# A two-layer graph network on one core: GpSimd gathers rows for phase two in the pause between the phases, from a list split by how early a row is ready

## The reference

```python
# layer 0: attention over the edges that enter a node
hi = x[src] @ w1;  hj = x[tgt] @ w2
logits = (leaky_relu(hi + hj, 0.3) * a).reshape(-1, 8, 16).sum(-1)
attn = softmax of logits over the edges with one tgt        # segment max, exp, segment sum
x = layernorm(x + segment_sum(hi * attn, tgt))
# layer 1: a message for every edge
ef = (relu(edge_attr @ We1 + be1) @ We2 + be2) * sigmoid(edge_weight * Wt + bt)
msg = relu(concat(x[src], ef) @ Wn1 + bn1) @ Wn2 + bn2
x = layernorm(x + (segment_sum(msg, dst) + x))
```

## Time and profile before

| | us |
|---|---|
| median of 3 runs | 2163.57 (2163.52, 2163.57, 2169.5) |
| the profiled execution | 2166.06 |
| its span in the trace | 2164.1 |
| GpSimd busy | 1585.8 (73%), 1679 instructions |
| TensorE matmul busy | 1630.1 (75%) |
| VectorE busy | 1312.3 (61%) |
| ScalarE busy | 645.3 (30%) |

### The profile page before, as it was taken

How to read it: one execution, slowest core, us unless ns; L and a number is a source line. 1 busy time by engine, 2 the same in 40 slices (tenths; PEclk the granted TensorE clock), 3 DMA queues, 4 the chain that set the end, 5 groups by cost and what they waited for, 6 DMA issues and landing times.

```text
span 2164.1 us, 39852 instructions
## 1 busy us (share of the span) xinstructions
PE 1630.1 (75%) x10499; PEld 1256.3 (58%) x10500; DVE 1312.3 (61%) x3313; ACT 645.3 (30%) x1376; POOL 1585.8 (73%) x1679
## 2 busy tenths in 40 slices
PE   5766766766676766766678778888888888888886
PEld 5554544545454554544556566666666666666665
DVE  5766667666776676767643355555555555555554
ACT  5211111111111111111133444344444344444442
POOL 6777777777777777777547777777777777777775
PEclk8999989899999899999989988988988988888897
DMA  8633333333333333333354344444444444444441
GB/s 261 150 86 86 84 96 91 95 86 96 97 86 96 88 93 92 94 94 89 88 165 140 126 127 143 129 138 132 128 144 128 130 142 128 142 130 141 129 130 45
DMA packets 145935, 252.48 MB, mean 117 GB/s; under 512 B 34549, under 2 KB 80874, under 8 KB 145882
## 3 DMA queue, kind: packets, MB, share of 16 engines
q1 hardware_dynamic: 92122, 142.56, 20.3%
q0 software_dynamic: 53184, 109.03, 19.4%
q10 hardware_dynamic: 576, 0.25, 0.1%
HBM read 233.91 MB, written 13.02 MB: 114 GB/s over the span
## 4 chain that ended last, share of the span: by engine, by line
POOL 59%; issue 23%; DVE 6%; PE 6%; DMA 3%; DVEq 1%; POOLq 1%; ACT 1%; SPq 0%; ACTq 0%
POOL T L712 33%; POOL G L680 26%; DMA G<-hi_rows,idx 2%; PE ps L1789 1%; PE ps L1812 1%; PE ps L1784 1%; DMA T<-y_rows,idx 1%; DVE msg L1285 1%; PE ps L1742 1%; DMA accF<-in_x_turned 1%; DVE oh L1338 0%; ACT V L848 0%; DVE V L1257 0%; DVEq L1262 0%; DVE G L1600 0%
## 5 line engine op out<-in xcount | busy, mean ns | idle before, releaser
L712 POOL DMA_INDIRECT T<-y_rows,idx x831 | 787.7, 948 | 295.4 <-issue 292.1
L680 POOL DMA_INDIRECT G<-hi_rows,idx x819 | 781.7, 954 | 261.1 <-issue 245.5
L1784 PE MATMUL ps<-ident,G 128*128 128x128 f32 x828 | 143.1, 299 | 287.0 <-DMA G<-hi_rows,idx 182.2
L2014 PE MATMUL ps<-wA,G 128*128 128x128 f32 x1664 | 266.1, 310 | 97.6 <-DVE T L1556 97.3
L949 ACT ACTIVATE G<-G 128x512 f32<-128x512 f32 x208 | 131.1, 630 | 595.7 <-DVE G L1600 594.2
L2014 PEld LDWEIGHTS ps<-wA,G 128*128 128x128 f32 x1664 | 232.3, 216 | 103.3 <-DVE G L1604 103.2
L848 ACT ACTIVATE V<-ps 128x512 f32<-128x512 f32 x207 | 123.7, 597 | 561.5 <-PE ps L1789 553.1
L1784 PEld LDWEIGHTS ps<-ident,G 128*128 128x128 f32 x828 | 94.9, 150 | 337.1 <-issue 298.1
L1596 DVE TENSOR_TENSOR G<-iotaF,R 128x256 f32<-128x256 f32 x208 | 88.6, 426 | 296.8 <-DMA T<-y_rows,idx 292.7
L1812 PE MATMUL ps<-msg,oh 128*128 128x137 f32 x1608 | 264.8, 313 | 0.3 <-issue 0.3
L1257 DVE TENSOR_TENSOR V<-ps,V 128x512 f32<-128x512 f32 x207 | 142.0, 686 | 201.6 <-ACT V L848 199.6
(11 more groups left out here) (201 smaller groups left out, 1701.5 us busy)
## 6 DMA issues: line engine op xcount, KB each, us to landing
T<-in_edge_weight_padded SPq DMA_DIRECT2D x104, 512.0 KB
T<-in_edge_attr_turned SPq DMA_DIRECT2D x104, 256.0 KB
Dbc<-block_destinations SPq DMA_DIRECT2D x69, 384.0 KB, 3.8
T<-y_rows,idx POOLq DMA_INDIRECT x831, 2.5
G<-hi_rows,idx POOLq DMA_INDIRECT x819
link<-scan_destinations SPq DMA_DIRECT2D x280, 16.1 KB
accF<-in_x_turned SPq DMA_DIRECT2D x7, 448.0 KB, 8.6
hi_rows<-T SPq DMA_DIRECT2D x12, 256.0 KB, 5.2
```

The costliest lines, as they stand in the source:

```text
L680: pool.indirect_dma_start(out=G[:, s, t * C:(t + 1) * C], out_offset=None, in_=hi_d[:, :], in_offset=bass.IndirectOffsetOnAxis(ap=idx[:, s ...
L712: pool.indirect_dma_start(out=Yb[:, r, t * C:(t + 1) * C], out_offset=None, in_=y_d[:, :], in_offset=bass.IndirectOffsetOnAxis(ap=idx[:, r ...
L1784: pe.matmul(U[j][:, i * P:(i + 1) * P], G[:, s, t * C:(t + 1) * C], ident[:, :], is_transpose=True, start=(i == 0), stop=False, skip_group ...
L2014: ins = pe.matmul(zP[i][:, n * C:(n + 1) * C], efS[i][:, n * P:(n + 1) * P], wN1[:, 1, :], start=True, stop=True)
```

## The change

It has three parts.

**The gathers.** y of batches 0 to 13, the first 42 blocks (`FIRM` = 5376 rows), is stored twice, in `y_rows` and in a table of its own, `firm_rows`. After the last sums of phase one (`s_u`) GpSimd gathers for the first seven quads (`KQ` = 7) from `firm_rows` with the plain list of sources and a bound: a row with a source of 5376 or more is skipped. When all of y is stored it goes over the same seven quads once more with a second list, `idxL`, in which the sources below 5376 are replaced by 65536, beyond the bound, so that only the rows that were left out are copied. Of the 3584 sources of these seven quads 13.4% are 5376 or more, between 11 and 24 of 128 in a tile. The buffers `msgZ`, `ohZ`, `msgO` and `ohO` of the end of phase one move, because `Yb` is now written earlier.

**The start.** SP no longer loads all of `IDX` (832 columns) in the prologue but the 48 that groups 1 to 3 need; the other 784, `dstI` and the quads' bases, which were broadcast to all partitions by ScalarE's queue, are loaded in step 0 of phase one (`load_lists`), behind the first loads of that step and ahead of the first copies of T. `wA` is loaded after the lists for the scans. VectorE makes the lists of tiles (`lane`, `R64`) and `idxL` in step 1, clears the accumulator and makes `wC` in step 0 and prepares the tables `tabR` and `tabA` at the very start. TensorE's product with `mean` moves ahead of the branch.

**The end of phase one.** The sums of the last quad (`last_sums`) stand behind the third window sum of that step. The moments of batch 14 are taken between the scans; its y and normalised rows are computed before the last window sum is added, not after; the sums of group O go to the other PSUM bank, so that TensorE need not wait for the addition before.

```diff
+            def load_lists():
+                sp.wait_ge(s_es, 16)
+                sp.dma_start(IDX[:, RG * GT:4 * NQ], srcT[:, RG * GT:4 * NQ]).then_inc(s_es, 16)
+                sp.dma_start(dstI, dstT).then_inc(s_td, 16)
+                sp.dma_start(baseB, baseI.rearrange("(o q) -> o q", o=1).to_broadcast([P, NQ])).then_inc(s_td, 16)
...
                     sp.dma_start(rows_of(y_d, m), mYb).then_inc(s_n["stored"], 16)
+                    if not is_int(m) or m < MC - 1:
+                        sp.dma_start(rows_of(firm_d, m), mYb).then_inc(s_n["stored"], 16)
...
-                pool.wait_ge(s_n["stored"], 16 * (MC + 1))
-                for q in range(RB):
+                def gather_part(q, rows, bound, table):
+                    for t in range(4):
+                        pool.indirect_dma_start(
+                            out=Yb[:, q, t * C:(t + 1) * C], out_offset=None, in_=table[:, :],
+                            in_offset=bass.IndirectOffsetOnAxis(ap=rows[:, 4 * q + t:4 * q + t + 1], axis=0),
+                            bounds_check=bound, oob_is_err=False).then_inc(s_gy[q], 16)
+                pool.wait_ge(s_u, NQ)
+                pool.wait_ge(s_n["stored"], 32 * (MC - 1))
+                for q in range(KQ):
+                    gather_part(q, IDX, FIRM - 1, firm_d)
+                pool.wait_ge(s_n["stored"], 32 * (MC - 1) + 32)
+                for q in range(KQ):
+                    pool.wait_ge(s_gy[q], 64)
+                    gather_part(q, idxL, NB * P - 1, y_d)
+                for q in range(KQ, RB):
                     gather_y(q, q)
...
                     leaky(0)
                     nxt(0)
+                    if is_int(g) and g == 0:
+                        dve.memset(acc[:, 0, 0:NP // 2], 0.0).then_inc(s_zero, 1)
+                        dve.wait_ge(s_odd_s, 2)
+                        dve.tensor_tensor(wC[:, :], wN1[:, 0, :], ps[7][:, P:2 * P], ALU.subtract)
+                        dve.wait_ge(s_gx["kept"], GQ)
+                        settled(dve.tensor_copy(lanes, iotaF[:, :]))
+                    if is_int(g) and g == 1:
+                        lists_of_tiles()
+                        dve.wait_ge(s_es, 32)
+                        settled(dve.tensor_scalar(idxL[:, :], IDX[:, 0:4 * KQ], float(FIRM), float(SKIP), ALU.is_lt, ALU.mult))
+                        settled(dve.tensor_tensor(idxL[:, :], idxL[:, :], IDX[:, 0:4 * KQ], ALU.max))
...
                     aggregate(1)
-                    if is_int(g) and g == NG - 2:
-                        last_sums()
                     if b is not None:
                         pe.wait_ge(s_r3, b + 1)
                         pe.matmul(shp[0:BR, 1:2], up[0:BR, 0:BR], R3[0:BR, 0:1], start=True, stop=True).then_inc(s_sh2, 1)
                     aggregate(2)
+                    if is_int(g) and g == NG - 2:
+                        last_sums()
```

More of the change, by code:

```diff
@@ L63 @@
 MN = NB - MC * MB
+KQ = 7
+FIRM = (MC - 1) * MB * P
+SKIP = 65536
 assert NODES <= 16384 and NO_NODE & 16384
@@ L113, in build @@
         idx = sb("idx", [P, RG, GT], I32)
[L114 to L115 removed]
+        idxL = sb("idxL", [P, 4 * KQ], I32)
+        tabs = sb("tabs", [65, NQ], I32)
+        baseR, tabR, tabA = tabs[0:1, :], tabs[32:33, :], tabs[64:65, :]
         ident = sb("ident", [P, P])
@@ L747, in _ @@
             act.dma_start(W12[:, :], w12).then_inc(s_w, 16)
-            act.dma_start(cols[:, :], vectors).then_inc(s_col, 16)
-            act.dma_start(bases[:, :], baseI.rearrange("(o q) -> o q", o=1).to_broadcast([P, NQ])).then_inc(s_row, 16)
+            for row in (baseR, tabR, tabA):
+                act.dma_start(row, baseI.rearrange("(o q) -> o q", o=1)).then_inc(s_row, 16)
+            act.dma_start(cols[:, :], vectors).then_inc(s_row, 16)
             def keep_hi(u):
@@ L874, in step @@
                     if f is not None and (not is_int(f) or f + RG < NG):
+                        if is_int(f) and f == 0:
+                            act.wait_ge(s_es, 32)
                         stage_idx(f + RG, s)
+                    if b is not None:
+                        act.wait_ge(s_xm, b + 1)
+                        need(act, s_ext, b)
+                        act.activation(EXT[0:BR, :], XM[0:BR, :], ACT.Exp).then_inc(s_exp, 1)
                     if is_int(g) and g == NG - 2:
@@ L980, in _ @@
             dve.memset(msgX[:, :, C:C + 1], 1.0).then_inc(s_fill, 1)
+            dve.memset(mean[:, :], 1.0 / C).then_inc(s_fill, 1)
             dve.memset(accF[:, BLANK:(2 * NB + 1) * RC], 0.0).then_inc(s_fill, 1)
@@ L1672, in _ @@
             pe.wait_ge(s_flag, 1)
+            pe.wait_ge(s_fill, 4)
+            pe.wait_ge(s_col, 16)
+            pe.matmul(ps[7][:, P:2 * P], mean[:, :], wN1[:, 0, :], start=True, stop=True).then_inc(s_odd_s, 1)
             with pe.If(pe.value_load(unusual[0:1, 0:1], min_val=0, max_val=1) > 0):
@@ L1923, in _ @@
                 ins.then_inc(s_n["xT"], 1)
-                hold(1, U[2])
+                carry_down(Z, shZ)
                 ready(A, 0)
                 sum_up(A, 0, msgX, oh)
-                carry_down(Z, shZ)
+                carry_up(Z, shZ)
                 ready(A, 1)
                 sum_up(A, 1, msgX, oh)
-                carry_up(Z, shZ)
+                carry_down(O, shO)
+                pe.wait_ge(s_msg, A + GQ)
+                turned_exp(Z, EXp)
                 ready(A, 2)
                 sum_up(A, 2, msgX, oh)
-                pe.wait_ge(s_msg, A + GQ)
-                turned_exp(Z, EXp)
-                carry_down(O, shO)
+                carry_up(O, shO)
+                ready(Z, 0)
+                sum_up(Z, 0, msgZ, ohZ)
+                turned_exp(O, EXO)
+                ready(Z, 1)
+                sum_up(Z, 1, msgZ, ohZ)
+                ready(Z, 2)
+                sum_up(Z, 2, msgZ, ohZ)
                 pe.wait_ge(s_n["xTc"], MC)
```

116 lines of the change are left out of this document (50 added, 66 removed).

## The result

The changed kernel takes 2170.06 us (median of 15 runs, 2165.93 to 2172.04), the kernel before 2165.3 us on the same chip (15 runs, 2162.88 to 2169.5). The ratio is 1.002, with a 95% interval from 1.0013 to 1.0026: about 5 us slower, 3 to 6 us by the interval. That is a real loss, and it lies within the 0.3% that the prediction calls no change. The forecast was 2144.7 us, its range ended at 2162. The profiled execution took 2171.27 us around a span of 2169.2 us, 5.1 us more than before.

A forecast was written before the change was run, and what follows sets the result against it. GpSimd's gathers were taken to bound both phases. The start's 2.5 us and the gathers' 16.4 us summed to 18.9 us, giving 2144.7 us from 2163.57, with a range of 2133 to 2162.

The forecast's parts named there:

- What bounds the kernel: GpSimd's gathers set the end of both phases; in phase two 831 gathers start 1.253 us apart without a break.
- The gathers: Around the pause between phases: two lists of 28 gathers end at 1125.3 instead of 1141.7, 16.4 us earlier.
- the middle of the first two: Assumed price of a split gather, between fully row-dependent and fully fixed work: 1.18 us first list, 0.84 us second.
- The bounds: Split gather's price: 1.12 and 0.43 us if work follows rows, 1.25 if fixed, up to 0.49 more for the check.
- The prediction's first rival: In the split lists, skipped rows save nothing; equal gather means were cited as fitting a fixed price; chance 22%.
- A skipped row costs what a copied one does: Split lists at full price: second list ends at 1139.0, 2.7 us earlier; time 2158.4 us with the start; chance 22%.
- The check makes each gather dearer: All 56 split gathers pay for the bound; a loss from 0.09 us each, 2175 us at 0.3 us; chance 13%.
- The end of phase one: Between phase one's last gather and y's store, reordered VectorE work removes waits: 5.5 us, stores landing at about 1100.
- the prediction's signs: If right, the last store of y comes some 35.7 us after phase one's last gather instead of 41.3.
- The start: In the prologue, GpSimd starts about 3.4 us earlier, but earlier first messages count: 2.5 us gain, range 0 to 4.5.

The follow-up runs named there:

- e6: Changed kernel with plain gathers for all quads once y is stored, no split lists, both new orders kept: 2158.75 us, ratio 0.9975 to the kernel before.
- e7: Kernel before with only the new order at the end of phase one, prologue and gathers as before: 2160.46 us, ratio 0.9982.
- e8: Kernel of e6 with a bound that skips nothing on all 831 gathers of phase two: 2202.21 us, ratio 1.0181 to the kernel before.
- e13: Changed kernel with three quads instead of seven in the split, 12 gathers in each list: 2159.75 us, ratio 0.9978 to the kernel before.
- e3: Changed kernel with first list skipping practically all rows and second copying all: 3230.36 us at the lower clock, ratio 1.0069 to the kernel before.
- e9: Kernel of e6 with the list loads issued behind the first copies of T instead of ahead: 2160.91 us, ratio 0.9984 to the kernel before.
- e1: Same kernel as e6, run at the lower clock: 3207.95 us, ratio 0.9996 to the kernel before.

## Why the prediction was wrong

**What bounds the kernel** was read rightly. GpSimd's groups still run without a break on both sides of the pause, and what e6, e7, e8 and e13 moved on its timeline came out at the end, give or take the up to 3.4 us by which the same stretch of gathers differs between executions.

**The gathers: the step that failed.** It is the choice of "the middle of the first two, half of the work fixed and half by rows", a period of 1.18 us for a gather of the first list and 0.84 for the second. From 1070.08 to 1108.72 the first took 1.38 us each, from there to 1145.58 the second 1.32. That is 5.6 and 13.3 us more than forecast. Of the first list's 1.38 us, 1.253 are the period of any gather, 0.05 the bound, and 0.08 the five long ones among the 28, which together took 2.15 us more than 1.00 each. The list also began 3.8 us later than the step had it (1066.3 with the start's gain): 1.2 us of the start's gain weren't there, the last sums themselves lie 6.4 us behind the last gather for 4.65 before, because the change puts them behind the third window sum, and 0.8 us pass between their end and the first gather. 5.6 + 13.3 + 3.8 + 1.3 for the stretch behind quad 7 is 24.0, the distance between −18.9 and +5.1. Of the 5.6 and 13.3 us together, 13.6 are the saving that skipped rows were given and don't have (56 gathers at 1.253 us for the 56.5 us forecast), and 5.3 come from the bound and the long gathers.

The bounds were open, and no row could have closed them. The prediction's first rival took the equal means of the earlier trace rows as a fit for a fixed price, but both groups there copy all 128 rows, so they fit a price by rows just as well. What the working could have shown is how little the split had to win at its other bound. At a fixed price it left 2.7 us for the pause, half of the 5.5 that it gave to the new order at the end of phase one alone, so that splitting the gathers undoes part of that order's gain. The comparison with the same kernel without the split wasn't made.

The rule of the Trainium skill, page "DMA: Bandwidth & Descriptors", section on the anatomy of a DMA on the gpsimd path, that descriptor generation is a small part and many descriptors go out before the cost shows, was set against the forecast there. The traces agree with it so far as they go: e3's two groups show the same 1.00 us at none and at all of 128 rows. Whether descriptors are written for a skipped row no run shows.

**The rivals.** "A skipped row costs what a copied one does" is what happened to the price. It gave 2158.4, since it left the bound free, took an end at 1139.0 and kept 2.5 us of the start. From its 5.2 us of gain to the measured +5.1 it is 10.3 us, and within rounding these are 3.8 for the later start of the first list, 1.3 behind quad 7 and 5.3 for dearer gathers. That last part is the second rival, "The check makes each gather dearer": the 56 took 75.5 us for 70.2, 0.095 us each, where its turning point to a loss was 0.09. The bound alone is 0.05, below that point, 2.9 of the 5.3 us; the rest are the long gathers. So neither rival alone gives the loss. What neither says is what the split does to the end's gain: their 56 gathers run on in one chain from the last sums, and then the stores no longer matter. Against the stores of the old order, after which gathers began at 1106.66, the first list would have overrun by about 2 us instead of 8.7, an estimate from the second list's start at 1108.72.

**The end of phase one** was right: the forecast was 5.5 us, the last store is 5.4 us nearer to the last gather, and the pause of e7 is 5.5 us shorter. From the end of the last gather to the landing of the store are 35.9 us for 41.2, where the prediction's signs had 35.7 for 41.3. The waits that were to go went, one by one. In the changed kernel this gain can't be used, since the first list holds GpSimd over it.

**The start** was sized at 2.5 us and gave 0.1 at group 4. The first gather came 4.1 us earlier for 3.4 forecast, but the stall took all of it, at the low end of the range of 0 to 4.5 us. The working named both things that held it: the load of destinations that the one-hot waits for until 76.88, and the 1.9 us of lists that come back in step 1. It weighed them in one sum with the gains and followed neither to its end. In the changed kernel the list work stands at 64.53 to 66.61 in VectorE's chain, whose last step ahead of the one-hot begins at 75.98 for 75.38 before, though the first sums are earlier; e9 and e8 show that shortening either chain alone leaves the messages where they are. Whether both together would free the start wasn't tried.

The 0.1 us itself isn't firm: in e7, whose start is that of the kernel before, the gather at group 4 comes at 81.14 for 79.69. At the last gather of phase one the five traces with the new start (the changed kernel, e6, e8, e9, e13) lie at 1061.25 to 1062.76, the two with the old one at 1063.33 and 1063.13, about 1.5 us apart in the mean. That is the table's −1.3, and in the changed kernel nearly all of it arises behind group 4: from there to its last gather it took 982.5 us and the kernel before 983.6.

**The version to keep** is e6: the new order at both ends with plain gathers, 2158.75 us, 0.25% below the kernel before and 0.45% below the changed one.

## What to carry to other kernels

Count what stays behind a barrier before filling the pause ahead of it. Where an engine's cost is per instruction, early work on a part of the data wins only if it removes instructions behind the barrier; here all 28 stayed and each became dearer. Compare such a change with the same kernel without that part, not only with the kernel before: the new orders alone were the better version. And when a change shortens a pause and fills it as well, price the filler against the new length: seven quads overran by 8.7 us what three left idle for 13.45. The middle of two bounds is no measurement. Where the whole gain hangs on a price that no row shows, measure it first; a bound on every gather (e8) was a change of one argument. And a stall can have two chains behind it that end together: follow both before the start ahead of it is given a gain.

## What the runs showed of the hardware

- An indirect gather of 128 rows of 512 bytes costs GpSimd about 0.95 us (means of 946 to 955 ns over some 800 gathers) and 0.30 us of issue, and a bound on its sources adds 0.052 us (43.5 us over 831 gathers). The cost doesn't depend on how many rows are skipped: 1.00 us at none, 13.4%, 86.6% and all of them copied.
- Single gathers at the end of phase one took 1.18 to 1.68 us for 1.00 in the changed kernel and up to 2.06 in e3, in a list that copies almost no rows. They occur at a DMA share of 0.00 as at 1.06, and begin beside a TENSOR_TENSOR of VectorE with both inputs in SBUF. The cause wasn't tested.
- The same kernel took 2165 us at a mean granted clock of 0.90 and 3117 to 3209 us at 0.73 to 0.75. The mean clock differs by a factor of 1.2, the time by 1.44 to 1.48, so the clock alone doesn't explain it. In e1, TensorE stands idle for 9.36 us up to 313.71 with no releaser in the profile, and 28% of the chain that ended last is put down to "another core or an unknown queue". GpSimd waits for the other engines there, and changes that are worth 0.2 to 0.3% otherwise don't show. What makes these executions slower stays open.
